# Decoder block with a 64-expert layer: adding an expert's rows to the result in two transfers, one a half of the tokens

## The chip, the cores and the metric

The kernel runs on one core of one Trainium2 chip, in one launch. The metric is the device time of that launch in microseconds; a kernel's time is the median of several runs. The trace is of one profiled execution, whose own time is given beside its span.

## The reference

The input `x` is eight sequences of 256 tokens of 512 floats (2048 tokens), all in float32. Three layers are added to it in turn: a windowed attention, a convolution that takes a second tensor, and a feed-forward layer of one shared pair of matrices and 64 experts. The change is in the last one:

```python
def _moe(x, idx, w, w1, w2):              # E = 64 experts, K = 6 a token, CAP = 128 slots
    T, D = x.shape
    e_flat = idx.reshape(-1)
    tok = jnp.repeat(jnp.arange(T), K)
    ...
    keep = pos < CAP                      # pos: how many earlier tokens chose this expert
    slot = jnp.where(keep, pos, CAP)
    xd = jnp.zeros((E, CAP + 1, D), x.dtype).at[e_flat, slot].set(x[tok])
    h = _relu2(jnp.einsum('ecd,eid->eci', xd, w1))
    yd = jnp.einsum('eci,edi->ecd', h, w2)
    y_assign = yd[e_flat, slot] * gate
    return jnp.zeros((T, D), x.dtype).at[tok].add(y_assign)
...
shared = _relu2(x @ shared_up_w.T) @ shared_down_w.T
return (shared + routed)
```

An expert takes the first 128 tokens that chose it. The routing of the given inputs, worked out with the reference itself, is very uneven: of the 64 x 128 = 8192 slots 3163 hold a token, 2734 of them one of tokens 0 to 1023 and 429 one of tokens 1024 to 2047. 29 experts have no token at all, 21 are full, and 17 are full with tokens below 1024 alone; 48 experts have none from 1024 up. The larger of an expert's two counts is 43.75 on the mean of the 64. The last two experts, 62 and 63, have 69 and 128 tokens below 1024, and 59 and 0 above.

## The kernel before

Attention, convolution and routing come first; the expert stage is the rest of the program, from about 575 us of the trace to its end. Each engine has its own program, and semaphores order them; nothing is scheduled by a compiler. Ahead of the stage VectorE makes `idxU`, a table with one column an expert: the token of each of its 128 slots, or, for an empty slot, T + slot, a row of the result that is thrown away. The stage runs over the 64 experts in order, in groups of 16 (`GROUP`), each group two rounds of eight (`UE`), with eight buffers for weights (`wring`) and gathered tokens (`xg`), and four (`NY`) for an expert's output rows (`ysb`).

For each expert:

- SyncE (SP) asks for its weights, 1 MB (`load_expert`, line 410). It does this six experts ahead (`AHEAD`).
- GpSimd (POOL) gathers its token rows from `xrows` (`gather`, line 563), eight experts ahead.
- TensorE (PE) transposes the rows (line 1615), multiplies by the first weights (`hidden`), and by the second (`outputs`, lines 1618 to 1633). In between it computes the shared layer for tokens 1024 to 2047, in four pieces of 256 tokens, one a group (`tile_part`, line 1653); the pieces are of different size, so an expert's share of PE's work repeats only every eight experts.
- VectorE (DVE) copies the expert's column of `idxU` into one of four columns of `idxs` (line 1306), one for the next gather into `idxg` (line 1307), and multiplies the product by the gates into `ysb` (line 1308). It waits until the adding transfer of four experts before has landed, which POOL tells it with `scatter_landed`.
- POOL adds the 128 rows to the result in HBM with an indirect transfer (`scatter`, line 574). One adding transfer must have landed before the next is issued, since two experts may hold the same token: POOL waits for `added`. After each, a small operation on `begun_mark` (line 579) counts `scatter_begun` up, on which SP's request for the weights of six experts later waits. Once a group, after the 15th expert, POOL also adds the shared layer's 256 rows (`scatter_tiles`, line 585), as another link of the same chain: `LINKS` = 17 a group.

PE's `outputs` of an expert waits until DVE has emptied the buffer two experts before. POOL works in the order of its program: scatter of expert n+1, mark, gather for expert n+8, scatter of expert n+2, and so on.

Of the kernel before, what the change touches and what calls it, by code (L numbers as in the profile page):

```python
# [6 lines left out]
P = 128  # L7
B, S, D = 8, 256, 512
T = B * S
NT = T // P  # L10
# [9 lines left out]
E, K, NG, TKG, CAP, I = 64, 6, 8, 4, 128, 256  # L20
# [41 lines left out]
def program(nc, a, out):  # L62
    f32, u32 = mybir.dt.float32, mybir.dt.uint32
    ALU, ACT, AX = mybir.AluOpType, mybir.ActivationFunctionType, mybir.AxisListType
    V, G, A, TE = nc.vector, nc.gpsimd, nc.scalar, nc.tensor
    ds = bass.ds
# [6 lines left out]
    with ctx:  # L73
        def sb(name, shape, dt=f32):
            return ctx.enter_context(nc.sbuf_tensor(name, shape, dt))

        def sem(name):
            return ctx.enter_context(nc.semaphore(name))
# [12 lines left out]
        minus_half = sb("minus_half", [P, NT])  # L91
# [5 lines left out]
        idxs = sb("scatter_rows", [P, 4], u32)  # L97
        idxt = sb("tile_scatter_rows", [P, 1], u32)
        tile_rows = sb("tile_rows", [P, NT // 4])
        begun_mark = sb("begun_mark", [P, 1])  # L100
        AREA = 34400
        arena = sb("arena", [P, AREA])
        place = [0]
# [165 lines left out]
        added = sem("rows_added_to_the_result")  # L269
        scatter_landed = sem("scatter_landed")  # L270
        scatter_begun = sem("scatter_descriptors_written")
        out_written = sem("result_rows_begun")
        upper_written = sem("upper_result_rows_begun")

# [81 lines left out]
        def _(sp):  # L356
# [13 lines left out]

            for s in (*empt, *conv_used, *conv_filled, *y_filled, *y_ready, hsq_ready, tile_ready):
                sp.sem_inc(s, 1)
            sp.sem_inc(scatter_landed, 5)
            sp.sem_inc(conv_done, 2)
            sp.sem_inc(x_loaded, 16)

# [32 lines left out]
            def load_expert(s, i):  # L409
                sp.dma_start(wring[s], a["wexp"][ds((i * UE + s) * P, P), :]).then_inc(wexp_loaded[s], 16)  # L410

            for s in range(UE):
                if s == 4:

                    sp.wait_ge(upper_written, 16)
                if s == 6:
                    sp.wait_ge(full[FS.bank(("dn", 1, 3))], FS.filled(("dn", 1, 3)))
                if s >= AHEAD:
                    sp.wait_ge(scatter_begun, s - AHEAD + 1)
                load_expert(s, 0)  # L420
            with sp.Fori(1, E // UE) as i:
                for s in range(UE):

                    sp.wait_ge(scatter_begun, i * UE + (s - AHEAD + 1))
                    load_expert(s, i)

            sp.wait_ge(added, 16 * (E + NT // 4))


        @block.gpsimd  # L430
        def _(pool):
# [133 lines left out]

            def scatter(s, i, before):
# [12 lines left out]
            def scatter_tiles(j):  # L581
                pool.wait_ge(tile_ready, j + 2)
                pool.wait_ge(added, j * (16 * LINKS) + 16 * (GROUP - 1))
                pool.sem_inc(scatter_landed, 1)
                pool.indirect_dma_start(out.rearrange("(r g) d -> r (g d)", g=2),
                                        bass.IndirectOffsetOnAxis(ap=idxt[:, 0:1], axis=0),
                                        ytile.rearrange("p g d -> p (g d)"), None, compute_op=ALU.add)\
                    .then_inc(added, 16)

            last = E // GROUP - 1  # L590
            for s in range(UE):
# [1 line left out]

            pool.wait_ge(upper_written, 16)
            pool.wait_ge(out_written, 16 * 2)
            scatter(0, 0, None)

            def group(j, more):
                for r in range(GROUP):
                    n = r + 1  # L600
                    if n == GROUP - 1:
                        scatter_tiles(j)
                    if n < GROUP:
                        scatter(n % UE, j * 2 + n // UE, j * (16 * LINKS) + 16 * (n if n < GROUP - 1 else n + 1))
                    elif more:
                        scatter(0, j * 2 + 2, j * (16 * LINKS) + 16 * LINKS)
                    if more or r < UE:
                        gather(r % UE)

# [171 lines left out]
        def _(dve):  # L781
# [502 lines left out]
            def experts(j, g, more):  # L1284
                i = j * 2 + g
                for s in range(UE):
                    r = g * UE + s
                    if s < UE - 1:
                        hidden_squared(s + 1, i)
                    elif more:  # L1290
                        hidden_squared(0, i + 1)
                    if s == UE - 1:

                        dve.wait_ge(full[7], FE.filled(("tile_dn",), i))
                        if g == 0:
                            dve.wait_ge(scatter_landed, j * LINKS + NY)
# [443 lines left out]
```

## Time and profile before

| | |
|---|---|
| median of 3 runs | 998.89 us (996.33 to 1003.96) |
| profiled execution, its own time | 995.25 us |
| its span, first to last instruction | 993.4 us |
| TensorE matmul busy | 892.7 us (90%) |
| VectorE busy | 564.3 us (57%) |
| GpSimd busy | 450.9 us (45%) |
| ScalarE busy | 232.5 us (23%) |
| 64 scatters on GpSimd (line 574) | 101.8 us busy, 208.6 us idle before them |
| 64 marks on GpSimd (line 579) | 50.8 us |

"Idle before" is time in which the engine had nothing to run just ahead of that group. A matmul's end is modelled, so that PE's busy time is not work at its peak. The time around the span is 995.25 - 993.4 = 1.85 us.

### The profile page before, as it was taken

The numbers are of one execution on the slowest core, as the hardware profiler recorded it, in microseconds if no ns is written. First come the engines' busy times: TensorE is split into PE (matmuls) and PEld (weight loads), VectorE is DVE, ScalarE is ACT, GpSimd is POOL, SyncE is SP. The second block draws the span as 40 slices with busy tenths as digits, with TensorE's granted clock in tenths as the row PEclk, the third lists the DMA queues.
The fourth block names the chain that finished last, engine by engine and source line by source line (L and its number), as shares of the span: only waits on it lengthen the run. The fifth ranks groups of instructions, "written<-read, shape, count | busy, mean of one in ns | idle before, by whom it ended". The sixth has DMA issues, their size and how long they took to land. (4 is left out here: it accounts for less than half of the span.)

```text
span 993.4 us, 14519 instructions
## 1 busy us (share of the span) xinstructions
PE 892.7 (90%) x4913; PEld 627.3 (63%) x4913; DVE 564.3 (57%) x1148; ACT 232.5 (23%) x716; POOL 450.9 (45%) x499
## 2 busy tenths in 40 slices
PE   4799999988899999869998999999899899998990
PEld 3566666664677777766443376868586668575850
DVE  4788878867688888876999722223233223222220
ACT  1455656461400000123110011111111111111110
POOL 1644452533588888620160134444445445344432
PEclk9989999999999999979999999999999999998995
DMA  7300000020533333033070158988998899789963
GB/s 290 112 1 2 1 2 1 2 75 1 210 105 100 96 92 92 0 128 128 0 275 0 60 177 259 270 254 222 290 277 259 220 271 290 214 225 298 275 149 53
DMA packets 44125, 143.40 MB, mean 144 GB/s; under 512 B 7280, under 2 KB 11632, under 8 KB 35120
## 3 DMA queue, kind: packets, MB, share of 16 engines
q1 hardware_dynamic: 26352, 96.46, 26.4%
q0 software_dynamic: 14912, 37.76, 19.4%
q10 hardware_dynamic: 2816, 8.59, 2.3%
q8 instruction: 27, 0.44, 0.2%
q14 instruction: 18, 0.15, 0.0%
HBM read 114.36 MB, written 28.43 MB: 144 GB/s over the span
## 5 line engine op out<-in xcount | busy, mean ns | idle before, releaser
L1346 PE MATMUL ps<-arena 128*128 128x128 f32 (+4 forms) x2128 | 521.1, 403 | 13.6 <-DVE arena L791 5.7
L1346 PEld LDWEIGHTS ps<-arena 128*128 128x128 f32 x2128 | 340.9, 192 | 156.7 <-issue 111.9
L574 POOL DMA_INDIRECT out<-arena,scatter_rows x64 | 101.8, 1590 | 208.6 <-DMA out<-arena,scatter_rows 144.3
L1281 DVE TENSOR_TENSOR arena<-arena 128x256 f32<-128x256 f32 x64 | 27.3, 427 | 221.3 <-ACT arena L776 208.3
L1346 PE MATMUL ps<-features_T,arena 128*128 (+2 forms) x640 | 116.0, 338 | 0.0
L624 ACT ACTIVATE arena<-ps 128x512 f32<-128x512 f32 (+1 forms) x137 | 78.3, 590 | 134.9 <-issue 63.0
L1346 PEld LDWEIGHTS ps<-features_T,arena 128*128 128x128 f32 x640 | 84.7, 188 | 37.3 <-issue 37.3
L563 POOL DMA_INDIRECT arena<-token_rows,gather_rows x64 | 66.9, 1046 | 64.1 <-DVE gather_rows L1274 52.9
L465 POOL TENSOR_TENSOR arena<-arena 128x512 f32<-128x512 f32 x48 | 49.2, 1057 | 87.6 <-DVE arena L811 87.6
L776 ACT ACTIVATE arena<-ps 128x256 f32<-128x256 f32 x64 | 24.6, 384 | 247.1 <-PE ps L1346 231.1
L634 ACT ACTIVATE arena<-arena 128x128 f32<-128x128 f32 x192 | 74.0, 389 | 16.6 <-DVE arena L799 16.3
L518 POOL TENSOR_TENSOR arena<-arena 128x512 f32<-128x512 f32 x32 | 40.7, 1272 | 43.2 <-DVE arena L1057 43.2
L1615 PEld LDWEIGHTS ps<-ident,arena 128*128 128x128 f32 x256 | 31.2, 142 | 44.1 <-DMA arena<-token_rows,gather_rows 23.4
L1653 PE MATMUL ps<-arena 128*128 128x512 f32 x128 | 57.5, 592 | 0.0
L1615 PE MATMUL ps<-ident,arena 128*128 128x128 f32 x256 | 39.6, 279 | 17.3 <-DMA arena<-token_rows,gather_rows 16.4
L579 POOL TENSOR_TENSOR begun_mark<-minus_half 128x1 f32<-128x1 f32 x64 | 50.8, 793 | 0.0
L1308 DVE TENSOR_SCALAR arena<-ps,arena 128x512 f32<-128x512 f32 x64 | 47.9, 748 | 0.0
L1306 DVE COPY scatter_rows<-slot_rows_u 128x1 uint32 (+1 forms) x64 | 9.8, 154 | 64.1 <-PE ps L1346 51.4
L1653 PEld LDWEIGHTS ps<-arena 128*128 128x128 f32 x128 | 24.3, 190 | 30.6 <-issue 30.6
L734 ACT ACTIVATE arena<-features_T 128x256 f32 x32 | 13.0, 416 | 122.0 <-DVE arena L1057 119.9
L1064 DVE TENSOR_REDUCE arena<-arena 128x1024 f32 (+1 forms) x32 | 38.6, 1206 | 0.0
L634 ACT ACTIVATION_READ_ACCUMULATOR arena<-arena 128x1 f32 x192 | 36.3, 189 | 0.0
(173 smaller groups left out, 1069.5 us busy)
## 6 DMA issues: line engine op xcount, KB each, us to landing
arena<-wexp SPq DMA_DIRECT2D x48, 1024.0 KB
residual<-wexp SPq DMA_DIRECT2D x16, 1024.0 KB
arena<-toeplitz_rows SPq DMA_DIRECT2D x32, 256.0 KB, 3.1
arena<-ctxE SPq DMA_DIRECT2D x32, 192.0 KB, 3.2
residual<-x SPq DMA_DIRECT2D x4, 1024.0 KB, 5.3
token_rows<-arena SPq DMA_DIRECT2D x16, 256.0 KB, 2.0
arena<-suT ACTq DMA_DIRECT2D x1, 2048.0 KB, 7.9
arena<-sdT ACTq DMA_DIRECT2D x1, 2048.0 KB, 12.6
```

The lines of the kernel that those rows point to most:

```text
L465: G.tensor_tensor(e, e, rinv[:, b, 4 * c:4 * c + 4, q:q + 1].broadcast_to((P, 4, P)), ALU.mult)\
L518: G.tensor_tensor(halfsum[:, s % 2].rearrange("p m j k -> p (m j) k"), pv[:, :, 0:4], pv[:, :, 4:8], ALU.add).then_inc(half_ready, 1)
L563: pool.indirect_dma_start(xg[:, s, :], None, xrows, bass.IndirectOffsetOnAxis(ap=idxg[:, s:s + 1], axis=0))\
L574: pool.indirect_dma_start(out, bass.IndirectOffsetOnAxis(ap=idxs[:, s % NY:s % NY + 1], axis=0), ysb[:, s % NY, :], None, compute_op=ALU.a ...
L579: G.tensor_tensor(begun_mark[:], minus_half[:, 0:1], minus_half[:, 0:1], ALU.mult).then_inc(scatter_begun, 1)
L624: A.activation(dst, src, ACT.Copy, **kw).then_inc(empt[bank], 1)
L634: ins = A.activation(prob[:, b, k, q, :], prob[:, b, k, q, :], ACT.Exp, bias=negmax[:, b, k, q:q + 1], scale=1.0, accum_out=rowsum[:, b, k ...
L1064: V.tensor_reduce(o[:, 0:2 * B, :], prodb[:, s % 2, 0:2 * B], axis=AX.X, op=ALU.add)
L1308: V.tensor_scalar(ysb[:, s % NY, :], ps[:, 4 + s % 2, :], xg[:, s, ds(i * UE + (D + s), 1)], None, ALU.mult)\
L1346: ins = TE.matmul(out_ap, lhsT, rhs, start=(n == 0), stop=(n == len(pairs) - 1))
L1615: ins = TE.transpose(ps[:, bank, c * P:(c + 1) * P], xg[:, s, c * P:(c + 1) * P], ident[:])
L1653: ins = TE.matmul(ps[:, 7, :], htile[:, k, :], sdT[:, k, :], start=(k == 0), stop=(k == 7))
```

## The change

Each expert's 128 slots are now given to two adding transfers. The lower one has the tokens of the expert as they are and a limit of 1023; the upper one has a second table, `idxV`, in which each token below 1024 has 2T added to it, and a limit of 2047. Of each, the slots whose index is over the limit are to be skipped (`oob_is_err=False`); an empty slot, T + slot, is over both. Each half has its own counts: `added[0]` and `landed[0]` for the lower rows, `added[1]` and `landed[1]` for the upper ones, and the shared layer's transfer is a link of the upper chain alone, as its rows are all from 1024 up. `begun_mark` and `scatter_begun` are gone. SP asks for weights when the upper transfer of seven experts before has landed (and the shared one, where it stands between), where it waited until the scatter of six experts before had been begun. DVE makes the table `idxV` once and copies one more column an expert.

```diff
-            sp.sem_inc(scatter_landed, 5)
+            sp.sem_inc(landed[0], NY)
+            sp.sem_inc(landed[1], NY + 1)
...
-                if s >= AHEAD:
-                    sp.wait_ge(scatter_begun, s - AHEAD + 1)
+                if s == AHEAD:
+                    sp.wait_ge(y_filled[0], 2)
+                elif s > AHEAD:
+                    sp.wait_ge(added[1], 16 * (s - AHEAD))
                 load_expert(s, 0)
-            with sp.Fori(1, E // UE) as i:
-                for s in range(UE):
-
-                    sp.wait_ge(scatter_begun, i * UE + (s - AHEAD + 1))
-                    load_expert(s, i)
...
+            def links_before(r):
+                return r + (1 if r == GROUP - 1 else 0)
...
+            with sp.Fori(0, E // GROUP - 1) as j:
+                for r in range(GROUP):
+
+                    late = r - AHEAD
+                    links = LINKS + links_before(late) if late >= 0 else links_before(GROUP + late)
+                    sp.wait_ge(added[1], j * (16 * LINKS) + 16 * links)
+                    load_expert(r % UE, j * 2 + (2 + r // UE))
...
-                if before is not None:
-                    pool.wait_ge(added, before)
-                    pool.sem_inc(scatter_landed, 1)
-                pool.indirect_dma_start(out, bass.IndirectOffsetOnAxis(ap=idxs[:, s % NY:s % NY + 1], axis=0),
-                                        ysb[:, s % NY, :], None, compute_op=ALU.add).then_inc(added, 16)
-
-                if before is not None:
-                    pool.wait_ge(scatter_begun, i * UE + s)
-                G.tensor_tensor(begun_mark[:], minus_half[:, 0:1], minus_half[:, 0:1], ALU.mult).then_inc(scatter_begun, 1)
+                for h in range(2):
+                    if upper is not None:
+                        pool.wait_ge(added[h], upper if h else n * 16)
+                        pool.sem_inc(landed[h], 1)
+                    pool.indirect_dma_start(halves[h], bass.IndirectOffsetOnAxis(ap=idxs[:, h, s % NY:s % NY + 1], axis=0),
+                                            ysb[:, s % NY, :], None, bounds_check=(T // 2 - 1, T - 1)[h], oob_is_err=False,
+                                            compute_op=ALU.add).then_inc(added[h], 16)
...
+            below, above = ysb[:, 0, 0:E], ysb[:, 1, 0:E]
+            V.tensor_copy(above, idxU[:, 0:E])
+            V.drain()
+            V.tensor_scalar(below, above, float(T // 2), float(2 * T), ALU.is_lt, ALU.mult)
+            V.drain()
+            V.tensor_tensor(above, above, below, ALU.add)
+            V.drain()
+            V.tensor_copy(idxV[:], above)
...
-                    dve.wait_ge(scatter_landed, j * LINKS + (r + 1 if r < NY - 1 else r + 2))
+                    dve.wait_ge(landed[0], i * UE + (s + 1))
+                    dve.wait_ge(landed[1], j * LINKS + (r + 1 if r < NY - 1 else r + 2))
                     dve.wait_ge(xg_loaded[s], i * 16 + 16)
 
-                    V.tensor_copy(idxs[:, s % NY:s % NY + 1], idxU[:, ds(i * UE + s, 1)])
+                    V.tensor_copy(idxs[:, 0, s % NY:s % NY + 1], idxU[:, ds(i * UE + s, 1)])
+                    V.tensor_copy(idxs[:, 1, s % NY:s % NY + 1], idxV[:, ds(i * UE + s, 1)])
```

On POOL, from the start of the loop over the groups, the program before reads so (`rows_added_to_the_result` is `added`, `scatter_descriptors_written` is `scatter_begun`, `expert_rows` is `y_ready`):

```order
L572 ISA [waits expert_rows1_ready]
L574 DMA out<-arena,scatter_rows 2176x512 [waits rows_added_to_the_result]
L578 ISA
L579 TENSOR_TENSOR begun_mark<-minus_half 128x1 [waits scatter_descriptors_written]
L563 DMA arena<-token_rows,gather_rows 128x576
L572 REGISTER_ALU [waits expert_rows2_ready]
L574 DMA out<-arena,scatter_rows 2176x512 [waits rows_added_to_the_result]
```

and at the same place the changed one (the two halves' counts are `added[0]` and `added[1]`):

```order
L587 ISA [waits expert_rows1_ready]
L589 DMA out<-arena,scatter_rows 1024x512 [waits rows_added_to_the_lower_half]
L587 ISA
L589 DMA out<-arena,scatter_rows 2048x512 [waits rows_added_to_the_upper_half]
L575 DMA arena<-token_rows,gather_rows 128x576
L587 ISA [waits expert_rows2_ready]
L589 DMA out<-arena,scatter_rows 1024x512 [waits rows_added_to_the_lower_half]
```

The mark's place is taken by a second adding transfer with a wait of its own, and the gather stands behind both.

On SP, the requests for the weights of experts 6 and 7 before the change:

```order
L410 DMA arena<-wexp 128x2048 [waits scatter_descriptors_written,bank5_filled]
L410 DMA arena<-wexp 128x2048 [waits scatter_descriptors_written]
```

and after it, from expert 6 on:

```order
L410 DMA arena<-wexp 128x2048 [waits expert_out_slot0_filled,bank5_filled]
L410 DMA arena<-wexp 128x2048 [waits rows_added_to_the_upper_half] x5
L410 DMA residual<-wexp 128x2048 [waits rows_added_to_the_upper_half] x2
```

The same requests stand in the same order; each now waits for a landing instead of an issue.

## Rows read from the trace of the kernel before

**Rows 1.** View by windows, expert stage cut at each eighth expert.

```profile
core 0: us, PE busy (x) PEld busy (x) DVE busy (x) ACT busy (x) POOL busy (x), PEclk, DMA share, GB/s
...
675.40:725.60 50.20, 47.52 (x274) 34.87 (x274) 13.31 (x36) 8.28 (x18) 22.04 (x24) 0.97 0.88 253
725.60:771.30 45.70, 45.70 (x275) 33.93 (x274) 13.34 (x37) 8.28 (x18) 23.22 (x24) 1.00 0.89 263
771.30:824.60 53.30, 47.70 (x274) 35.33 (x274) 13.33 (x36) 8.28 (x18) 24.69 (x25) 0.97 0.88 252
824.60:872.50 47.90, 45.92 (x271) 33.34 (x270) 13.28 (x37) 8.28 (x18) 20.43 (x22) 1.00 0.85 252
872.50:927.80 55.30, 48.48 (x274) 35.86 (x273) 12.19 (x37) 8.28 (x18) 27.04 (x28) 0.94 0.90 257
```

**Rows 2.** Who waited for whom, 584 to 994 us: total, times, longest.

```profile
POOL out L574 <- DMA out<-arena,scatter_rows: 144.3, 48, 6.9
...
PEld ps L1615 <- DMA arena<-token_rows,gather_rows: 23.4, 9, 6.3
...
POOL out L574 <- DMA out<-arena,tile_scatter_rows: 15.9, 3, 5.7
```

**Rows 3.** Timeline of POOL, two links of the chain at 731 us.

```profile
731.02 1.59 POOL L574 DMA_INDIRECT out<-arena,scatter_rows  x1 [2.48 <-DMA out<-arena,scatter_rows]
732.05 0.78 POOL L579 TENSOR_TENSOR begun_mark<-minus_half 128x1 f32<-128x1 f32 x1
732.99 1.02 POOL L563 DMA_INDIRECT arena<-token_rows,gather_rows  x1 [0.16 <-issue]
736.55 1.59 POOL L574 DMA_INDIRECT out<-arena,scatter_rows  x1 [2.53 <-DMA out<-arena,scatter_rows]
```

**Rows 4.** By tile, scatter_rows: the 64 experts' adding transfers.

```profile
DMA to landing us min/median/max: 4.4/4.8/9.4
```

**Rows 5.** By tile, tile_scatter_rows: the four transfers of 512 KB.

```profile
DMA to landing us min/median/max: 5.9/6.0/6.5
```

**Rows 6.** Timeline of PE, 785 to 812 us.

```profile
787.91 1.88 PE L1346 MATMUL ps<-arena 128*128 128x512 f32 x4
794.02 1.09 PE L1615 MATMUL ps<-ident,arena 128*128 128x128 f32 x4 [4.23 <-DMA arena<-token_rows,gather_rows]
794.90 3.20 PE L1346 MATMUL ps<-arena,residual 128*128 128x128 f32 x16
```

**Rows 7.** Timeline of POOL, the first gathers back to back.

```profile
569.79 0.95 POOL L563 DMA_INDIRECT arena<-token_rows,gather_rows  x1 [0.30 <-issue]
571.05 0.95 POOL L563 DMA_INDIRECT arena<-token_rows,gather_rows  x1 [0.30 <-issue]
```

**Rows 8.** View by windows, stretches inside one expert's period.

```profile
727.50:729.50 2.00, 2.00 (x20) 2.00 (x19) 0.00 (x0) 0.60 (x1) 1.03 (x1) 1.00 1.02 141
729.50:731.50 2.00, 2.00 (x15) 1.62 (x14) 0.07 (x1) 0.49 (x2) 0.48 (x1) 1.00 1.03 424
727.00:732.65 5.65, 5.65 (x41) 4.64 (x41) 0.42 (x1) 1.47 (x3) 3.00 (x5) 1.00 0.95 292
```

**Rows 9.** Timeline of DVE, the last shared addition.

```profile
574.43 0.69 DVE L1247 TENSOR_TENSOR residual<-residual,ps 128x512 f32<-128x512 f32 x1 [7.21 <-PE ps L1346]
```

**Rows 10.** The page's costliest groups: DVE's index copies.

```profile
L1306 DVE COPY scatter_rows<-slot_rows_u 128x1 uint32 (+1 forms) x64 | 9.8, 154 | 64.1 <-PE ps L1346 51.4
```

**Rows 11.** Timeline of the end, DVE and POOL, last two experts.

```profile
961.71 0.74 DVE L1308 TENSOR_SCALAR arena<-ps,arena 128x512 f32<-128x512 f32 x1
...
966.86 0.74 DVE L1308 TENSOR_SCALAR arena<-ps,arena 128x512 f32<-128x512 f32 x1
...
974.67 1.56 POOL L574 DMA_INDIRECT out<-arena,scatter_rows  x1 [3.89 <-DMA out<-arena,scatter_rows]
...
980.22 1.56 POOL L585 DMA_INDIRECT out<-arena,tile_scatter_rows  x1 [3.76 <-DMA out<-arena,scatter_rows]
986.96 1.56 POOL L574 DMA_INDIRECT out<-arena,scatter_rows  x1 [5.18 <-issue]
```

More of the change, by code:

```diff
@@ L96, in program @@
         idxg = sb("gather_rows", [P, 8], u32)
-        idxs = sb("scatter_rows", [P, 4], u32)
+        idxV = sb("upper_slot_rows_u32", [P, E], u32)
+        idxs = sb("scatter_rows", [P, 2, 4], u32)
         idxt = sb("tile_scatter_rows", [P, 1], u32)
         tile_rows = sb("tile_rows", [P, NT // 4])
-        begun_mark = sb("begun_mark", [P, 1])
         AREA = 34400
@@ L268, in program @@
         tile_ready = sem("shared_tile_ready")
-        added = sem("rows_added_to_the_result")
-        scatter_landed = sem("scatter_landed")
-        scatter_begun = sem("scatter_descriptors_written")
+        added = [sem("rows_added_to_the_lower_half"), sem("rows_added_to_the_upper_half")]
+        landed = [sem("lower_rows_landed"), sem("upper_rows_landed")]
         out_written = sem("result_rows_begun")
@@ L417, in _ @@
                     sp.wait_ge(full[FS.bank(("dn", 1, 3))], FS.filled(("dn", 1, 3)))
-                if s >= AHEAD:
-                    sp.wait_ge(scatter_begun, s - AHEAD + 1)
+                if s == AHEAD:
+                    sp.wait_ge(y_filled[0], 2)
+                elif s > AHEAD:
+                    sp.wait_ge(added[1], 16 * (s - AHEAD))
                 load_expert(s, 0)
-            with sp.Fori(1, E // UE) as i:
-                for s in range(UE):
-                    sp.wait_ge(scatter_begun, i * UE + (s - AHEAD + 1))
-                    load_expert(s, i)
-            sp.wait_ge(added, 16 * (E + NT // 4))
+            def links_before(r):
+                return r + (1 if r == GROUP - 1 else 0)
+            for r in range(UE, GROUP):
+                sp.wait_ge(added[1], 16 * links_before(r - AHEAD))
+                load_expert(r % UE, 1)
+            with sp.Fori(0, E // GROUP - 1) as j:
[4 more added lines that the diff above has]
+                    load_expert(r % UE, j * 2 + (2 + r // UE))
+            sp.wait_ge(added[0], 16 * E)
+            sp.wait_ge(added[1], 16 * (E + NT // 4))
         @block.gpsimd
@@ L564, in gather, with scatter @@
                     .then_inc(xg_loaded[s], 16)
-            def scatter(s, i, before):
+            halves = (out[0:T // 2, :], out[0:T, :])
+            def scatter(s, i, n, upper):
                 pool.wait_ge(y_ready[s % NY], i * (UE // NY) + (s // NY + 2))
-                if before is not None:
-                    pool.wait_ge(added, before)
-                    pool.sem_inc(scatter_landed, 1)
-                pool.indirect_dma_start(out, bass.IndirectOffsetOnAxis(ap=idxs[:, s % NY:s % NY + 1], axis=0),
-                                        ysb[:, s % NY, :], None, compute_op=ALU.add).then_inc(added, 16)
-                if before is not None:
-                    pool.wait_ge(scatter_begun, i * UE + s)
-                G.tensor_tensor(begun_mark[:], minus_half[:, 0:1], minus_half[:, 0:1], ALU.mult).then_inc(scatter_begun, 1)
+                for h in range(2):
[5 more added lines that the diff above has]
+                                            compute_op=ALU.add).then_inc(added[h], 16)
             def scatter_tiles(j):
                 pool.wait_ge(tile_ready, j + 2)
-                pool.wait_ge(added, j * (16 * LINKS) + 16 * (GROUP - 1))
-                pool.sem_inc(scatter_landed, 1)
-                pool.indirect_dma_start(out.rearrange("(r g) d -> r (g d)", g=2),
+                pool.wait_ge(added[1], j * (16 * LINKS) + 16 * (GROUP - 1))
+                pool.sem_inc(landed[1], 1)
+                pool.indirect_dma_start(halves[1].rearrange("(r g) d -> r (g d)", g=2),
                                         bass.IndirectOffsetOnAxis(ap=idxt[:, 0:1], axis=0),
                                         ytile.rearrange("p g d -> p (g d)"), None, compute_op=ALU.add)\
-                    .then_inc(added, 16)
+                    .then_inc(added[1], 16)
             last = E // GROUP - 1
@@ L595, in _ @@
             pool.wait_ge(out_written, 16 * 2)
-            scatter(0, 0, None)
+            scatter(0, 0, 0, None)
             def group(j, more):
@@ L600, in group @@
                     n = r + 1
+                    link = n if n < GROUP - 1 else n + 1
                     if n == GROUP - 1:
                         scatter_tiles(j)
[L603 to L606, printed above, removed]
+                    if n < GROUP or more:
+                        scatter(n % UE, j * 2 + n // UE, j * GROUP + n, j * (16 * LINKS) + 16 * link)
                     if more or r < UE:
@@ L1295, in experts @@
                         if g == 0:
-                            dve.wait_ge(scatter_landed, j * LINKS + NY)
+                            dve.wait_ge(landed[1], j * LINKS + NY)
                         V.tensor_copy(ytile[:, g, :], ps[:, 7, :]).then_inc(empt[7], 1)
```

## The prediction

> **What bounds the kernel now.** I read the view by windows first, cut at each eighth expert, because PE's work for an expert is uneven but repeats every eight [rows 1]. The octet from 725.6 to 771.3 us is clean: PE is busy all 45.7 us at a granted clock of 1.00. So PE asks for 45.7 us an octet, 5.71 us an expert. The other four rows are longer, by 4.5, 7.6, 2.2 and 9.6 us, 23.9 us together, and in the worst the granted clock falls to 0.94. The list of waits says what PE missed there: gathered rows, 23.4 us in nine waits, and no wait for weights stands in it; POOL at the same time waits 144.3 us for adding transfers and 15.9 us for the shared one [rows 2]. The timeline of PE shows one such place: it stands 4.2 us before the transposes at 794.02, and the first matmuls after that take 3.20 us for what takes 1.95 elsewhere in the same view at full clock [rows 6].
>
> Why gathers are late is seen in POOL's timeline [rows 3]. Scatter, mark, gather, then 2.5 us of nothing until the last scatter has landed: 736.55 - 731.02 = 5.53 us for a link. A landing takes 4.8 us on the median, and the rest of the link, 0.73 us (0.74 in the shared one's 6.74, below; I take 0.8), passes from it to the next issue [rows 4], so a link is 5.5 to 5.6 us. The shared transfer is a link of 986.96 - 980.22 = 6.74 us [rows 11], of which 6.0 are the landing [rows 5]. Sixteen experts cost the chain 16 x 5.6 + 6.7 = 96.3 us where PE needs 2 x 45.7 = 91.4. Two octets in a row took 95.9 and 101.2 us [rows 1], that is what the chain says plus transfers that landed late (up to 9.4 us). **The chain of adding transfers sets the pace,** by 5 to 10 us in a group, and PE is right behind it. The gather stands behind the waiting scatter in POOL's program, which is how the chain reaches PE. The mean of the four middle octets is 49.3 us, 6.16 us an expert.
>
> **What the change removes and adds.**
>
> *The mark* goes: 0.78 us of POOL, whose cover was the wait for the landing. By itself it is worth nothing. The second issue takes its place. The nearest rows for what an issue holds POOL: the mark starts 1.03 us after the issue [rows 3], so 1.03 at least; at most the 1.59 that is shown and the 0.30 that stands between gathers, 1.89. A gather behind another takes 1.26 us [rows 7]. POOL's own work per expert becomes 2 x 1.03 to 2 x 1.89 plus 1.26, 3.3 to 5.0 us, below 5.71. I take the upper end, 5.0, since two issues with a wait between are nearer to that. No row shows an issue with a limit that skips rows; see the rivals.
>
> *The chain* becomes two, but POOL's order ties them: lower n, upper n, gather, lower n+1. Each half must still wait for its own landing, so two chains by themselves would bring nothing: a link remains a landing plus 0.8. What can bring something is that a half has fewer rows. By the routing the larger half has 43.75 of 128 rows on the mean, and the empty slots go out altogether. What rows cost in a landing: the shared transfer has twice the bytes (512 KB) and lands in 6.0 us against 4.8 [rows 4, 5], so 1.2 us per 256 KB. By that a landing falls to 4.8 - 1.2 x (84.25 / 128) = 4.0 us; its bounds are 3.6 (no row) and 4.8 (the number of rows doesn't matter, or the transfer meets other traffic). A link is then 4.8 us (4.4 to 5.6), a group 16 x 4.8 + 6.8 = 83.6 us, against 91.4 of PE. With four row buffers between DVE and POOL the 17 full experts (5.6 each) are evened out. The limit at which the chain still keeps up is a link of (91.4 - 6.8) / 16 = 5.3 us. So **PE becomes the bound.**
>
> *The DMA engines.* While 128 rows are being added, the share is 1.02 with only 141 GB/s; while weights come, 1.03 with 424 [rows 8]. Added rows are the dearest bytes here: 2.0 us of all 16 engines for one expert, of 0.95 x 5.65 = 5.4 us in a period. If skipped rows are free, 3163 of 8192 remain, 0.8 us, and the period needs 4.1 us of 5.71.
>
> *Weights on the landed count.* Before, SP's request follows the issue of a scatter by 1.8 us (the mark that releases it ends then [rows 3]); now it follows the landing of the upper rows of the expert before, which is about 0.8 us ahead of the same place's issue. It comes some 2.6 us earlier against the chain. Nothing is queued on SP behind it but the next request. The slack: expert s is asked for about 8 us after DVE has taken expert s-7 (issue 2, second issue 2, landing 4), and PE wants it 5.3 experts, 30 us, after that point; 1 MB at 424 GB/s is 2.5 us of transfer. 20 us remain, so no gain and no loss from PE's side. Its price is that weights may now run beside an adding transfer, which is in the upper bound of a landing above.
>
> *DVE* gets one more copy an expert, 0.154 us [rows 10], and four small operations once. The copies are 10 us in all beside an engine that is busy 13 of 46 us [rows 1]; the four lie ahead of an addition before which DVE stood idle 7.2 us [rows 9]. Both cost nothing; without that cover they would cost 0.15 us an expert and about 1 us.
>
> **The sum.** From PE: 23.9 us, the four long octets. DVE takes expert 63 at 966.86 - 23.9 = 943.0 and expert 62 at 961.71 - 23.9 = 937.8 us [rows 11]. Then the tail: lower 62 issued at 939.4 and upper 62 at 941.3; landed with 69 rows after 4.2, at 945.5; shared transfer at 946.3, landed after 6.0 [rows 5] at 952.3; upper 63, without rows, at 953.1, landed after 3.6 at 956.7; and from the last landing (986.96 + 4.8) to the end of the span 1.6 us as now: 958.3. I add 0.7 for what is left of a queue. So a span of 959 and 961 us of own time (1.85 around it), 34 less than 995.25. The median of the runs shown is 3.6 us above that execution, so I forecast **964 us**. Its own range: 955 (landings of 3.6, no queue) to 972 (PE still loses 8 us in places).
>
> **Rivals.**
>
> *Links don't get short.* A landing's time may be mostly fixed (4.4 us is the least of 64 [rows 4]), or the weights, now running beside the adding transfers, give back what fewer rows gain. At 5.6 us a link a group takes 96.3 us against 98.6 (2 x 49.3) now: 2.3 us a group, 9 in all, and up to 20 where the late landings go too. That gives 979 to 990 us, 985 as a point. For it: the DMA share of 0.95 leaves little room. Against it: half of the transfers carry no row at all.
>
> *Skipped rows are carried by the DMA engines.* If a skipped row costs a share f of an added one, an expert needs 5.4 - 2.0 + 0.8 + 3.2 f = 4.2 + 3.2 f us of the engines (207 of 256 descriptors are skipped; 2.0 x 207 / 128 = 3.2). From f = 0.47 the engines hold PE up, from f = 0.6 they are slower than the 6.16 us of now. At f = 0.8 it is 6.8 us, 0.6 x 64 = 38 more: 1037 us; at f = 1, 1080. Against it: a row that is skipped moves no bytes; nothing in the trace shows one. The Trainium skill speaks against this change in this sense: "DMA: Bandwidth & Descriptors", section "Rules for kernel authors", says of two transfers to disjoint halves of the partitions not to bother, since both spray over the same 16 engines and serialize, and to use one. The trace agrees in so far as the engines are full in both stretches of [rows 8]; by that rule nothing is gained but what the skipped rows leave out.
>
> *The issue with a limit holds POOL longer.* If the comparison of the 128 indices with the limit falls to POOL, each issue is longer by it, twice an expert. POOL needs 2x + 1.26 us an expert; it passes PE's 5.71 at x = 2.2 and the 6.16 of now at x = 2.45. At twice the row's 1.59, 3.2 us, an expert takes 7.7 us: 1.5 x 64 = 97 us more, near 1095. Against it: gather and scatter with 128 indices take 0.95 to 1.59 us and seem to differ by little else than their kind.
>
> **How the numbers follow.** Forecast 0.64, links don't get short 0.14, skipped rows are carried 0.14, the long issue 0.08. A measurement of this kernel tells about 1%, 10 us, from no change. Faster by over that (below 989): 0.64 and 0.10 of the second case, 0.74. Within: 0.04 of it and 0.05 of the third, 0.09. Slower (over 1009): 0.09 and 0.08, 0.17. The range goes from 955, the forecast's own lower end, with 0.03 below, to 1009 with 0.17 above; the costly ends of the last two rivals lie outside.
>
> **What would show it.** In the profile after: every octet near 45.7 us with a granted clock of 1.00; no waits of PE for gathers; landings of lower and upper transfers of 3.6 to 4.8 us, shorter for experts without tokens; POOL idle ahead of the lower issue for DVE, not for a landing; DMA share near 0.75; last landing some 14 us after DVE has taken expert 63. Wrong would be: landings of 4.8 us or more in all experts (first rival), a DMA share near 1 with fewer GB/s (second), an issue far over 1.6 us and POOL without idle time (third).

## The result and the profile after

| | before | changed |
|---|---|---|
| median | 1000.78 us (4 runs, 996.33 to 1003.96) | 1026.03 us (4 runs, 1021.78 to 1027.81) |
| profiled execution's span | 993.4 us | 1026.0 us |
| expert 0 taken by DVE | 584.1 us | 593.7 us |
| expert stage from there to the end | 409.3 us | 432.3 us |

The changed kernel takes 1.0249 times as long (95% interval 1.0193 to 1.0306). The forecast was 964 us, in a range from 955 to 1009. Ratios of times here and below leave out executions more than 1.5% above the fastest of the same kernel, medians leave out none.

The view by windows of the changed kernel, cut where DVE takes each eighth expert, answers to [rows 1]:

```profile
639.40:685.00 45.60, 45.60 (x274) 33.83 (x273) 14.14 (x44) 8.28 (x18) 28.56 (x20) 1.00 0.71 219
685.00:738.00 53.00, 47.98 (x275) 35.31 (x274) 14.21 (x45) 8.28 (x18) 33.43 (x24) 0.97 0.74 215
738.00:790.00 52.00, 48.06 (x289) 35.40 (x289) 14.21 (x45) 8.28 (x18) 32.55 (x24) 1.00 0.77 225
790.00:847.70 57.70, 46.80 (x259) 33.96 (x258) 14.14 (x44) 8.28 (x18) 35.16 (x26) 0.94 0.75 214
847.70:899.00 51.30, 47.21 (x270) 34.56 (x269) 14.07 (x45) 8.28 (x18) 34.76 (x26) 0.97 0.69 228
899.00:954.70 55.70, 48.61 (x295) 35.93 (x294) 12.65 (x45) 8.28 (x18) 32.89 (x25) 1.00 0.72 210
```

The first row is clean, 45.6 us; the other five take 51.3 to 57.7, 53.9 us on the mean where [rows 1] have 45.7 to 55.3. The forecast had PE set the pace in every octet; in these five it doesn't, and it waits more than before. The DMA share is 0.69 to 0.77 where it was 0.85 to 0.90: the engines are freed, as forecast (near 0.75). The list of waits, beside [rows 2]:

```profile
POOL out L589 <- DMA out<-arena,scatter_rows: 84.1, 39, 4.8
...
PEld ps L1636 <- DMA arena<-token_rows,gather_rows: 51.4, 20, 7.8
...
POOL out L589 <- DMA out<-arena,tile_scatter_rows: 13.4, 4, 3.4
```

POOL waits less for landings (84.1 us for 144.3), but PE waits twice as long for gathers: 51.4 us for 23.4. The timeline of POOL shows two kinds of period, beside [rows 3]. First an expert with 128 lower rows (19) and what follows it, then one without any rows (35):

```profile
723.84 1.58 POOL L589 DMA_INDIRECT out<-arena,scatter_rows  x1 [2.60 <-DMA out<-arena,scatter_rows]
725.72 1.56 POOL L589 DMA_INDIRECT out<-arena,scatter_rows  x1 [0.30 <-issue]
727.58 1.02 POOL L575 DMA_INDIRECT arena<-token_rows,gather_rows  x1 [0.30 <-issue]
730.70 1.58 POOL L589 DMA_INDIRECT out<-arena,scatter_rows  x1 [2.09 <-DMA out<-arena,scatter_rows]
...
835.56 1.58 POOL L589 DMA_INDIRECT out<-arena,scatter_rows  x1 [3.37 <-DMA out<-arena,scatter_rows]
837.44 1.56 POOL L589 DMA_INDIRECT out<-arena,scatter_rows  x1 [0.30 <-issue]
839.30 1.02 POOL L575 DMA_INDIRECT arena<-token_rows,gather_rows  x1 [0.30 <-issue]
841.02 1.58 POOL L589 DMA_INDIRECT out<-arena,scatter_rows  x1 [0.70 <-issue]
```

730.70 - 723.84 = 6.86 us, ended by the landing of the lower transfer; before, a period was 5.53. And 841.02 - 835.56 = 5.46 us with nothing waited for: lower issue, 1.88, upper issue, 1.86, gather, 1.72. Over the stage POOL issues a lower transfer each 6.63 us ((1012.9 - 595.4) / 63).

The page's row of GpSimd's queue, and the last empty transfers, when no weights or gathers are asked for any more:

```profile
q0 software_dynamic: 24128, 27.57, 12.5%
```

```profile
990.57 1.55 POOL L589 DMA_INDIRECT out<-arena,scatter_rows  x1 [2.24 <-DMA out<-arena,scatter_rows]
992.43 1.55 POOL L589 DMA_INDIRECT out<-arena,scatter_rows  x1 [0.31 <-issue]
994.29 1.55 POOL L589 DMA_INDIRECT out<-arena,scatter_rows  x1 [0.30 <-issue]
```

Bytes are fewer (the page of before has 37.76 MB) and packets more (14912 before): 3163 of them carry a row of 2048 bytes, and 13221 = 2 x 8192 - 3163 are of 8 bytes, one for each skipped slot; below I call these empty descriptors. Their number, and each transfer's landing below (the time from its issue to the last of its updates), I read from the trace's records of DMA packets and semaphore updates; the views don't show the landings of this kernel, since some updates are missing. At 990.57 a lower transfer without rows landed in 2.62 us (its last update on record; a few tenths may be missing); the same kind in the middle of the stage took 4.3.

### The profile page after: what moved, and what is told of

It is laid out like the page before. It is cut to its first block and busy times, and to the rows that moved or that the text cites. A ratio compares the mean times of both kernels' runs of the same rounds, so it can differ in the third digit from the quotient of the medians.

```text
span 1026.0 us, 14884 instructions
## 1 busy us (share of the span) xinstructions
PE 903.8 (88%) x4913; PEld 635.9 (62%) x4913; DVE 571.5 (56%) x1216; ACT 232.6 (23%) x716; POOL 534.1 (52%) x499
## 5 line engine op out<-in xcount | busy, mean ns | idle before, releaser
L589 POOL DMA_INDIRECT out<-arena,scatter_rows x128 | 201.2, 1572 | 141.6 <-DMA out<-arena,scatter_rows 84.1
L477 POOL TENSOR_TENSOR arena<-arena 128x512 f32<-128x512 f32 x48 | 49.3, 1060 | 87.6 <-DVE arena L822 87.6
L1636 PEld LDWEIGHTS ps<-ident,arena 128*128 128x128 f32 x256 | 30.5, 143 | 67.4 <-DMA arena<-token_rows,gather_rows 51.4
L530 POOL TENSOR_TENSOR arena<-arena 128x512 f32<-128x512 f32 x32 | 40.7, 1272 | 44.0 <-DVE arena L1068 44.0
L516 POOL TENSOR_TENSOR arena<-arena 128x512 f32<-128x512 f32 x32 | 35.1, 1096 | 0.0
```

Source lines behind the costliest of these rows:

```text
L477: G.tensor_tensor(e, e, rinv[:, b, 4 * c:4 * c + 4, q:q + 1].broadcast_to((P, 4, P)), ALU.mult)\
L516: G.tensor_tensor(rows[:, :, :, 5:9], c[:, :, 0:4].unsqueeze(3).broadcast_to((P, M, 4, 4)), c[:, :, 4:8].unsqueeze(2).broadcast_to((P, M, ...
L530: G.tensor_tensor(halfsum[:, s % 2].rearrange("p m j k -> p (m j) k"), pv[:, :, 0:4], pv[:, :, 4:8], ALU.add).then_inc(half_ready, 1)
L589: pool.indirect_dma_start(halves[h], bass.IndirectOffsetOnAxis(ap=idxs[:, h, s % NY:s % NY + 1], axis=0), ysb[:, s % NY, :], None, bounds_ ...
L1636: ins = TE.transpose(ps[:, bank, c * P:(c + 1) * P], xg[:, s, c * P:(c + 1) * P], ident[:])
```

## The experiments

Three edits were made at once: empty and other slots are skipped, the rows are split in two transfers, and the weights are asked for on a landing. All six combinations are timed (the split needs the skipping). "One" is the single transfer of the kernel before. The stage is that of one profile each, from the moment DVE takes expert 0 to the end.

| | request on the issue | request on the landing |
|---|---|---|
| one, all rows | before: 999.11 us, stage 409.3 | 1046.26 us, stage 458.3 |
| one, skipping | 964.88 us, stage 374.5 | 992.67 us, stage 404.7 |
| two, skipping | 1005.33 us, stage 411.6 | changed: 1026.03 us, stage 432.3 |

The four kernels of the next four sections were timed beside the kernel before at 999.11 us. Those behind them, up to the mark ahead of the issue, were timed on another chip, where the kernel before took 1003.95 us; a difference from one set to the other is told by ratio and by stage, not by the plain times.

**Two transfers, request on the issue.** To the changed kernel the mark is given back, behind the two issues:

```diff
+                if upper is not None:
+                    pool.wait_ge(scatter_begun, i * UE + s)
+                G.tensor_tensor(begun_mark[:], minus_half[:, 0:1], minus_half[:, 0:1], ALU.mult).then_inc(scatter_begun, 1)
...
-                    sp.wait_ge(added[1], j * (16 * LINKS) + 16 * links)
-                    load_expert(r % UE, j * 2 + (2 + r // UE))
+                    sp.wait_ge(scatter_begun, i * UE + (s - AHEAD + 1))
+                    load_expert(s, i)
```

> The changed kernel, but the mark is back behind the two issues and SP asks for weights on it, as before the change. Theory 1 (the request on the landed count puts the weights' packets beside the adding transfers; in the changed kernel lower transfers without any row took 4.3 us where two at the very end, beside nothing, took 2.6 and 2.7, and full ones 6.1 against 4.8): landings fall back to 2.7 to 4.8 us, the expert stage becomes PE's, 965 to 985 us. Theory 2 (the second issue on POOL is what costs: 1.88 + 1.86 + 1.72 = 5.46 us at least an expert, 0.8 us more here for the mark, so 6.2): no better than 1015 us.

Measured: 1005.33 us (10 runs), 1.0035 times the kernel before (0.9987 to 1.0082). Neither theory alone: the request's place is worth 21 us, and 40 remain against the single skipping transfer. These 40 are not the split alone. The mark stands behind the second issue, so the request goes out 3.9 us behind an expert's first issue, on the median, where it is 2.0 in the kernels with one transfer and the request on the issue: it has come 1.9 us nearer to the next adding transfer.

**One transfer, all rows, request on the landing.**

```diff
-                if before is not None:
-                    pool.wait_ge(scatter_begun, i * UE + s)
-                G.tensor_tensor(begun_mark[:], minus_half[:, 0:1], minus_half[:, 0:1], ALU.mult).then_inc(scatter_begun, 1)
...
-                    sp.wait_ge(scatter_begun, i * UE + (s - AHEAD + 1))
-                    load_expert(s, i)
+                    sp.wait_ge(added, j * (16 * LINKS) + 16 * links)
+                    load_expert(r % UE, j * 2 + (2 + r // UE))
```

> The kernel before with one edit: no mark, and SP asks for weights on the landed count of the one chain. Theory 1: full landings go from 4.8 to 6 us or more, a link to 6.8, 64 experts to 435 us: 1030 to 1060 us. Theory 2: as before or up to 1% faster (POOL loses 0.8 us of work that was hidden), 990 to 1000 us.

Measured: 1046.26 us, 1.0476 times the kernel before (1.0399 to 1.0553). This edit alone, which I had priced at nothing, costs 47 us. By tile, scatter_rows, beside [rows 4]:

```profile
DMA to landing us min/median/max: 4.5/5.8/7.6
```

**One transfer that skips, request on the issue.**

```diff
-                pool.indirect_dma_start(out, bass.IndirectOffsetOnAxis(ap=idxs[:, s % NY:s % NY + 1], axis=0),
-                                        ysb[:, s % NY, :], None, compute_op=ALU.add).then_inc(added, 16)
+                pool.indirect_dma_start(out[0:T, :], bass.IndirectOffsetOnAxis(ap=idxs[:, s % NY:s % NY + 1], axis=0),
+                                        ysb[:, s % NY, :], None, bounds_check=T - 1, oob_is_err=False,
+                                        compute_op=ALU.add).then_inc(added, 16)
```

> The kernel before with one edit: the single adding transfer has a limit of 2047, so that empty slots are skipped (3163 of 8192 rows are left); the mark and the request stay. Both theories: landings of 2.7 us for an expert without rows and 4.8 for a full one, a mean link of 4.3 us, below PE's 5.7: about 960 to 970 us. If the skipped rows are what costs (a third theory: each is still a descriptor of 8 bytes), no better than 990 us.

Measured: 964.88 us, 0.9682 times the kernel before (0.9605 to 0.976). It beats both kernels. Its windows, landings and tail:

```profile
675.10:720.80 45.70, 45.70 (x274) 33.93 (x274) 13.32 (x37) 8.28 (x18) 23.14 (x24) 1.00 0.78 246
720.80:766.50 45.70, 45.70 (x275) 33.93 (x274) 13.39 (x38) 8.28 (x18) 21.75 (x23) 1.00 0.80 253
766.50:813.10 46.60, 46.03 (x274) 33.66 (x273) 13.22 (x36) 8.28 (x18) 24.32 (x25) 1.00 0.78 249
813.10:858.40 45.30, 45.30 (x272) 33.53 (x271) 13.26 (x38) 8.28 (x18) 25.75 (x28) 1.00 0.84 287
```

```profile
DMA to landing us min/median/max: 2.7/4.2/8.3
```

```profile
943.10 0.74 DVE L1309 TENSOR_SCALAR arena<-ps,arena 128x512 f32<-128x512 f32 x1
...
945.24 1.56 POOL L586 DMA_INDIRECT out<-arena,tile_scatter_rows  x1 [3.88 <-DMA out<-arena,scatter_rows]
...
951.83 1.56 POOL L574 DMA_INDIRECT out<-arena,scatter_rows  x1 [5.03 <-issue]
```

Octets of 45.3 to 46.6 us at a clock of 1.00: PE sets the pace. Of PE's waits for gathers little is left:

```profile
PEld ps L1616 <- DMA arena<-token_rows,gather_rows: 2.2, 2, 1.3
```

Expert 63 is taken at 943.10, where my sum had 943.0; the shared transfer is issued at 945.24 (946.3), the last one at 951.83 (953.1).

**One transfer that skips, request on the landing.** Both edits above.

> The kernel before with both edits: one adding transfer with the limit of 2047, no mark, weights asked for on the landed count. It differs from the changed kernel only in that the rows aren't split. Theory 1: slower than with the request on the issue by 3% or more, 1000 to 1025 us. Theory 2 (the split is what costs): close to the kernel with the skip alone, 960 to 975 us.

Measured: 992.67 us (10 runs), 0.9934 times the kernel before (0.9893 to 0.9975). 28 us lie between it and the kernel with the skip alone, a little under what theory 1 gave, and 33 between it and the changed kernel (28 by the stage), which theory 1 does not give. In both the request goes out at about the same place, 0.7 and 0.5 us ahead of the next expert's issue on the median. So the split has a price of its own.

**The second issue without the second chain.** To the kernel with one skipping transfer:

```diff
+                pool.indirect_dma_start(out[0:T, :], bass.IndirectOffsetOnAxis(ap=idxnone[:, 0:1], axis=0),
+                                        zeros[:], None, bounds_check=T - 1, oob_is_err=False,
+                                        compute_op=ALU.add).then_inc(nothing_added, 16)
```

> The kernel with one skipping transfer (964.9 us), and behind each a second adding transfer whose 128 indices are all over the limit, with a semaphore on which nothing waits before the end. It has the second issue and its 128 empty descriptors, but not the second chain. If POOL's issue and the descriptors are what the split costs: near the split kernel with the request on the issue, 995 to 1005 us. If the tie of two chains to each other is what costs: 965 to 975 us.

Measured: 999.24 us (10 runs), 0.9966 times the kernel before (0.9924 to 1.0008), against 0.9682 without the empty transfer: 28 us by the ratios, 33 by the stage (407.4 us for 374.5). Most of the split's 40 us are there, with no second chain at all, so the tie of the chains can be at most the rest. But the edit does two things: the mark now stands behind the second issue, and the request with it, again 3.9 us behind the first issue where it was 2.0.

**POOL's time alone.**

```diff
+                if before is not None:
+                    pool.wait_ge(busy_done, i * UE + s)
+                G.tensor_tensor(busy_rows[:], minus_half[:, 0:1].broadcast_to((P, 768)),
+                                minus_half[:, 0:1].broadcast_to((P, 768)), ALU.mult).then_inc(busy_done, 1)
```

> The kernel with one skipping transfer, and behind each mark an operation on POOL of 128x768 elements, 1.5 to 2 us as a second issue would be, without any transfer. If POOL's time alone is what the split costs: as slow as the kernel with the empty second transfer. If the descriptors cost (in the engines' queues, or by longer landings): within 1% of 965 us, since POOL needs 2.0 + 1.3 + 2 = 5.3 us of 5.7.

Measured: 978.23 us, 0.9697 times the kernel before (0.9614 to 0.9779). By the ratios that is 1.5 us more than without the operation, and the intervals overlap; by the stage (385.3 us for 374.5) it is 11. By octets, its profile keeps PE's pace but for one place, the second of these rows:

```profile
728.60:774.30 45.70, 45.70 (x274) 33.93 (x274) 19.14 (x37) 8.28 (x18) 32.28 (x31) 1.00 0.82 255
774.30:820.00 45.70, 40.86 (x237) 30.45 (x236) 12.78 (x27) 6.53 (x14) 30.20 (x28) 0.96 0.71 213
```

The operation is not POOL's time alone either: DVE is busy 19.1 us in the first row, where it was 13.3 without it. Timelines of POOL, this kernel and then the one with the empty second transfer:

```profile
759.13 1.60 POOL L576 DMA_INDIRECT out<-arena,scatter_rows  x1 [0.52 <-issue]
760.19 0.77 POOL L582 TENSOR_TENSOR begun_mark<-minus_half 128x1 f32<-128x1 f32 x1
760.33 2.03 POOL L586 TENSOR_TENSOR busy_rows<-minus_half 128x768 f32<-128x768 f32 x1
762.54 1.04 POOL L565 DMA_INDIRECT arena<-token_rows,gather_rows  x1 [0.17 <-issue]
```

```profile
761.60 1.59 POOL L577 DMA_INDIRECT out<-arena,scatter_rows  x1 [1.09 <-DMA out<-arena,scatter_rows]
763.50 1.55 POOL L580 DMA_INDIRECT out<-zeros,no_rows  x1 [0.30 <-issue]
764.51 0.78 POOL L586 TENSOR_TENSOR begun_mark<-minus_half 128x1 f32<-128x1 f32 x1
765.44 1.04 POOL L566 DMA_INDIRECT arena<-token_rows,gather_rows  x1 [0.16 <-issue]
766.78 1.59 POOL L577 DMA_INDIRECT out<-arena,scatter_rows  x1 [0.30 <-issue]
```

From the main issue to the gather POOL takes 762.54 - 759.13 = 3.41 us with the operation and 765.44 - 761.60 = 3.84 with the second issue, so the operation holds it 0.4 us less. Main transfers without rows landed in 2.9 us beside the busy operation, in 3.9 beside the empty second transfer. Two things can make that difference: the 128 empty descriptors, or the request, since the mark begins 1.06 us behind the main issue in the first timeline and 2.91 in the second. The packet records speak for the request. With the empty second transfer, 21 of the 29 main transfers without rows had 0.4 MB or more of weights' packets beside them (counted from 1 us behind the issue), with the busy operation 3, and without either 6; those with less than 0.1 MB beside them landed in 2.7 to 2.8 us in all three. No run has the second issue with the mark ahead of it, so how the cost divides between the two is not shown.

**The changed kernel with small weights.** The only one here that computes something else:

```diff
-                sp.dma_start(wring[s], a["wexp"][ds((i * UE + s) * P, P), :]).then_inc(wexp_loaded[s], 16)
+                w = 2048 if isinstance(i, int) and i == 0 else 256
+                sp.dma_start(wring[s][:, 0:w], a["wexp"][ds((i * UE + s) * P, P), 0:w]).then_inc(wexp_loaded[s], 16)
```

> The changed kernel, but from the second round of eight on only the first 256 of 2048 columns of an expert's weights are loaded (128 KB for 1 MB), at the same times; the other columns keep the first round's weights, so the experts' products are not those of the reference. Theory 1 (the weights' packets beside the adding transfers lengthen landings): lower transfers without rows fall from 4.3 to 2.7 us, full ones from 6.1 to 4.8, and the time to 965 to 985 us (POOL's 5.5 us an expert and the shared transfers remain). If it isn't the weights' packets but the early request or the second issue itself: landings stay, 1010 us or more.

Measured: 969.15 us, 0.9625 times the kernel before (0.9563 to 0.9687), with all issues, chains and waits of the changed kernel in place: 62 us less than that one by the ratios, 55 by the stage (377.2 us for 432.3). In POOL's timeline the same two issues and gather:

```profile
761.17 1.58 POOL L590 DMA_INDIRECT out<-arena,scatter_rows  x1 [1.48 <-DMA out<-arena,scatter_rows]
763.06 1.56 POOL L590 DMA_INDIRECT out<-arena,scatter_rows  x1 [0.30 <-issue]
764.92 1.02 POOL L576 DMA_INDIRECT arena<-token_rows,gather_rows  x1 [0.30 <-issue]
766.86 1.58 POOL L590 DMA_INDIRECT out<-arena,scatter_rows  x1 [0.92 <-DMA out<-arena,scatter_rows]
```

A period of 5.69 us with a transfer of 128 lower rows at its start (expert 29); such a period took 6.86 and 7.06 us for experts 19 and 29 of the changed kernel. So it is the weights' packets, beside which the adding transfers run, that make the changed kernel slow. This edit removes most of those packets and can't tell their number from their place; the place is told by the request's move, in three pairs above. And the stage is 3 us longer than that of the single skipping transfer with whole weights: without weights beside it, neither the second issue nor its empty descriptors cost much.

**The mark ahead of the issue.** The skipping single transfer, with the mark's three lines moved from behind the issue to ahead of it, behind the wait for the landing.

> The kernel with one skipping transfer, with the mark ahead of the issue in place of behind it: the request for weights still hangs on the mark, but goes out about 1.8 us earlier against the adding transfer, and the issue itself 0.9 us later. Theory 1 (it is a matter of when the weights' packets arrive): most of the loss of the request on the landed count is there, 980 to 995 us, with landings of empty transfers over 4 us. If what matters is that the request hangs on a landing: within 1% of 965 us.

Measured: 1015.24 us, 1.0104 times the kernel before (1.0042 to 1.0166), worse than I gave it, and 42 us more than with the mark behind by the ratios, 47 by the stage (421.2 us). The request hangs on the mark in both; its time differs, and the mark now stands in the chain. Timeline of POOL, and SP's request after the first of these rows:

```profile
762.57 0.19 POOL L575 TENSOR_TENSOR begun_mark<-minus_half 128x1 f32<-128x1 f32 x1 [3.47 <-DMA out<-arena,scatter_rows]
763.29 1.58 POOL L576 DMA_INDIRECT out<-arena,scatter_rows  x1 [0.53 <-issue]
765.18 1.02 POOL L563 DMA_INDIRECT arena<-token_rows,gather_rows  x1 [0.30 <-issue]
768.61 0.19 POOL L575 TENSOR_TENSOR begun_mark<-minus_half 128x1 f32<-128x1 f32 x1 [2.42 <-DMA out<-arena,scatter_rows]
```

```profile
762.94 0.33 SPq L410 DMA_DIRECT2D arena<-wexp  x1
```

The request goes out 0.35 us ahead of the issue, where it followed 2.0 us behind it. Empty transfers landed in 4.65 us on the median. The mark in the chain costs little: from a landing to the next issue 0.95 us pass on the median, 0.85 with the mark behind.

Medians of the landings, by what a transfer carries, in us (read from the semaphore updates; where some are missing, from the last on record, which can be some tenths too short; lower and upper where there are two):

| kernel | empty | 128 rows |
|---|---|---|
| one, skipping, request on the issue | 2.8 | 5.0 |
| the same, POOL busy | 2.9 | 4.9 |
| the same, empty second transfer | 3.9 | 5.4 |
| the same, mark ahead | 4.65 | 6.0 |
| one, skipping, request on the landing | 4.3 | 5.6 |
| two, request on the issue | 4.4, upper 2.8 | 5.8 |
| changed | 4.3, upper 3.9 | 6.1 |
| changed, small weights | 2.6, upper 2.7 | 4.9 |

**Both kernels once more,** one run each.

> The changed kernel once more, for where its time lies. In its first profile DVE took expert 0 at 593.7 us, 9.6 us later than in the profile of before (584.1), though nothing ahead of that point is changed but four small operations. If that is spread between executions: in some of this and the next run it is found at another place between 583 and 594 us in either kernel, and the stage behind it is 432 us again, as in the first. If the change caused it: 593 us or more here and 584 in the kernel before.

> The kernel before once more, unchanged, for the same question: expert 0 taken somewhere between 583 and 594 us if it is spread, at 584 if the change is the cause; the stage behind it 409 us, give or take 5.

Measured: the changed kernel 1027.32 us with expert 0 at 592.1 and a stage of 433.4 us; the kernel before 1005.03 us with expert 0 at 591.6 and 411.6. A third execution of the kernel before, beside these two, took 991.41 us. So the later start is spread between executions, not the change; what the change costs is the stage's 22 us. The view by windows from 430 to 460 us, before in its first profile and in this one:

```profile
430.00:460.00 30.00, 27.82 (x201) 25.64 (x202) 16.11 (x36) 10.64 (x18) 3.39 (x2) 0.85 0.47 174
```

```profile
430.00:460.00 30.00, 25.91 (x155) 25.71 (x156) 15.30 (x44) 7.80 (x14) 3.54 (x2) 0.61 0.38 141
```

The granted clock there was 0.85 in one execution and 0.61 in the other, of the same program. Both are means of full clock (2.4 GHz) and half (1.2 GHz): half was granted for 10 us in the first and for 24 in the second, after 6.5 us in which PE had been busy 0.6 and 2.1 us. Expert 0's time goes with it over all twelve profiles: the three with 0.85 took it at 583.8 to 584.2 us, the nine with 0.60 to 0.66 at 589.1 to 593.7. That is why stages are compared here.

## Why the prediction was wrong

*What bounds the kernel, right.* The chain of adding transfers sets the pace and PE is right behind: with landings made shorter and nothing else, PE's 45.7 us an octet and a total of 964.88 us came out, by the sum as written. That the total is within 1 us of 964 is partly luck: its executions spread from 960 to 969 us.

*The skipped rows, right.* Rows not carried gave 34 us (999.11 to 964.88). Each is still a packet of 8 bytes, but a single empty transfer landed in 2.7 us at best, below the 3.6 I took as the lower bound. The rows' share was mis-sized: I took 1.2 us for 128 rows from the shared transfer, and the medians are 2.8 us empty and 5.0 full, 2.2 apart. The rival that they fill the engines is refuted by a share of 0.69 to 0.77.

*Weights on the landed count: the step that failed.* I wrote "no gain and no loss from PE's side", which holds, since no wait for weights appears, and put the price into "the upper bound of a landing above", 4.8 us. That bound was too low: full lower transfers landed in 6.1 us, empty ones in 4.3, and where my sum had 83.6 / 16 = 5.2 us an expert, shared transfers included, it took 6.63. The late landings up to 9.4 us in [rows 4] showed what an adding transfer costs when it meets other traffic (in that trace the eight with less than 0.1 MB of weights' packets beside them landed in 4.7 us on the mean, the five with over 0.8 MB in 7.7, the 9.4 among them); I took them for accidents and bounded the new state, in which each one may meet it, by the median of the old, in which the request came 2.0 us behind the issue and the weights ran after the added rows, as the two stretches of [rows 8] show. By itself the edit costs 47 us with all rows, 28 with a single skipping transfer, 21 with two.

*The second issue, which I priced at nothing: mis-sized.* I took 5.0 us for POOL's work in an expert; it is 5.46 (1.88 + 1.86 + 1.72), since I left out the 0.4 us and more between the gather and the next issue. That is below 5.71, and the split still costs 33 us with the request on the landing and 40 with it on the issue, where I had it at nothing. A busy POOL alone gave 2 to 11 us. I take it that POOL, 0.25 us an expert faster than PE, cannot catch up after a shared or a full transfer, but that is argued, not tried. A second transfer without rows, on which nothing waits, cost 28 to 33 us, but in that kernel the request had moved 1.9 us as well, and the records of packets put at least part of the cost there; what the empty descriptors cost by themselves is open.

*The rival "links don't get short"* had the mechanism, weights beside adding transfers, at a chance of 0.14 and a price of 979 to 990 us. Its price was wrong: at 5.6 us it kept links no longer than now. Links of 6.86 us, and the mean of 6.63 an expert with the shared transfers in it, are longer than before, where that mean is 6.37 ((986.96 - 585.74) / 63).

*A slip without weight.* In the tail of the sum it is the upper transfer of expert 62 that holds up the shared one; it has 59 rows, not 69, which changes 0.1 us.

The Trainium skill advises against two transfers to disjoint halves of the partitions ("DMA: Bandwidth & Descriptors", "Rules for kernel authors"). Both transfers here name all 128 partitions, so this is a neighbouring case; in it, too, two were worse than one, by 33 us with the request at the same place. No row is carried twice, so the bytes are not what is paid twice.

Open: whether an empty descriptor waits its turn behind a large packet of the weights is what the landings suggest (2.7 us alone, 4.3 beside weights), but no run counted the turns. The mark ahead of the issue is 17 us worse than the request on the landing, by ratio and by stage, though that request goes out earlier still: 0.1 us a link is the mark in the chain, the rest are landings longer by 0.3 to 0.4 us, and why those are longer isn't explained. And how the split's 33 to 40 us divide among POOL's time, the empty descriptors, the request's place and the tie of the chains was not tried.

## What to carry to other kernels

A request's place against another transfer is a cost even if its data come early enough: when moving one, ask what it will now run beside, and price that with the longest landings in the trace, not the median. Split a mixed change in a table of its edits: here one of three is worth 34 us and the other two cost 61 together. Look at what an edit moves besides: a second issue put ahead of the mark also put the request off by 1.9 us, and so its price can't be told from the request's. Drop the rows that need not move before thinking about how to overlap them.

## What the hardware showed that I had not expected

An adding transfer of 128 skipped rows lands in 2.7 us alone and in 4.3 to 4.65 beside weights of 1 MB, so a transfer without rows is delayed by 1.6 to 2 us too. And the same program's granted clock from 430 to 460 us was 0.85 in one execution and 0.61 in another, and expert 0 was taken 7.5 us later.
